# A recommendation tower on one core: copies of 128 rows for the pair products, and squares in quarters of the array

## What is computed

```
conv1 = einsum('bid,bjd,ijk->bkd', e, e, W1)          # 39 x 39 pairs of features -> 128
hidden1, final1 = conv1[:, :64], conv1[:, 64:]
conv2 = einsum('bid,bjd,ijk->bkd', e, hidden1, W2)    # 39 x 64 -> 128
z = concat([final1, conv2], 1).sum(over d)            # 192 numbers a sample
h = relu(concat([z, dense_ctx]) @ W_top1 + b_top1)    # 208 -> 512
h = relu(h @ W_top2 + b_top2)                         # 512 -> 256
y = h @ W_top3
```

## Time and profile before

| | |
|---|---|
| median of three runs | 795.92 us (795.42 to 796.37) |
| span of the profiled execution | 794.7 us |
| busy: PE, DVE, ACT, POOL | 734.3, 700.8, 634.8, 541.0 us |
| TensorE's clock, mean granted | 0.989 |
| moved by DMA | 169 MB, 213 GB/s over the span |

### The profile page before, as it was taken

How to read it: one execution, slowest core, us unless ns; L and a number is a source line. 1 busy time by engine, 2 the same in 40 slices (tenths; PEclk the granted TensorE clock), 3 DMA queues, 4 the chain that set the end, 5 groups by cost and what they waited for, 6 DMA issues and landing times.

```text
span 794.7 us, 18326 instructions
## 1 busy us (share of the span) xinstructions
PE 734.3 (92%) x6944; PEld 419.2 (53%) x6944; DVE 700.8 (88%) x1142; ACT 634.8 (80%) x1573; POOL 541.0 (68%) x542
## 2 busy tenths in 40 slices
PE   1895869899999999999999999999999999999996
PEld 0552123445556464656556566546455645666576
DVE  6984979989999989999999998998989999999862
ACT  1332459788998988888989989897979889898973
POOL 6887777777777777777777777777777777720000
PEclk9998989999999999999999999999999999999999
DMA  6738888788889788888878896878878788878300
GB/s 194 229 85 268 245 203 237 222 222 227 230 232 261 209 228 241 218 237 236 237 217 247 239 273 169 256 198 242 238 214 252 203 234 242 231 205 255 127 2 2
DMA packets 130904, 168.99 MB, mean 213 GB/s; under 512 B 99144, under 2 KB 112182, under 8 KB 114080
## 3 DMA queue, kind: packets, MB, share of 16 engines
q1 hardware_dynamic: 110756, 156.62, 67.1%
q0 software_dynamic: 16896, 8.68, 7.1%
q10 hardware_dynamic: 3164, 2.52, 1.1%
HBM read 156.03 MB, written 16.71 MB: 217 GB/s over the span
## 4 chain that ended last, share of the span: by engine, by line
DMA 26%; PE 25%; DVE 24%; ACT 13%; SPq 7%; issue 4%; POOL 1%; ACTq 0%; DVEq 0%
DVE blocks L827 20%; DMA copies<-xt 16%; PE hidden L455 9%; DMA emb<-in_tbl,ids_tile 8%; ACT arena L670 6%; PE sums L482 4%; PE hidden L569 4%; SPq L361 4%; PE sums L508 3%; ACT xdiag L658 2%; ACT hid_high L639 2%; DVE turned L859 2%; PE sums L526 2%; SPq L332 2%; ACT copies L688 1%
## 5 line engine op out<-in xcount | busy, mean ns | idle before, releaser
L422 POOL DMA_INDIRECT emb<-in_tbl,ids_tile x528 | 537.8, 1019 | 160.9 <-issue 101.8
L827 DVE TENSOR_TENSOR blocks<-copies 117x512 f32<-117x512 f32 x840 | 524.5, 692 | 57.3 <-DMA copies<-xt 24.0
L455 PE MATMUL hidden<-blocks,w_pairs 117*64 117x512 f32 x1792 | 430.8, 605 | 20.2 <-DVE blocks L827 18.4
L670 ACT ACTIVATE arena<-sums 64x480 f32<-64x480 f32 (+2 forms) x936 | 293.0, 313 | 38.8 <-PE sums L482 24.7
L455 PEld LDWEIGHTS hidden<-blocks,w_pairs 117*64 117x64 f32 x1792 | 144.5, 137 | 231.3 <-DVE blocks L827 113.9
L482 PEld LDWEIGHTS sums<-xdiag,turned 64*103 64x103 f32 x2000 | 99.3, 168 | 90.2 <-issue 54.7
L482 PE MATMUL sums<-xdiag,turned 64*103 64x78 f32 x2000 | 112.9, 257 | 13.2 <-ACT arena L670 10.9
L658 ACT ACTIVATE xdiag<-turned 32x468 f32<-32x468 f32 (+1 forms) x256 | 118.9, 464 | 3.1
L688 ACT ACTIVATE copies<-copies 117x2048 f32<-117x2048 f32 x32 | 61.2, 1912 | 54.4 <-DMA copies<-xt 34.9
L508 PE MATMUL sums<-arena,weights 128*64 128x128 f32 x1280 | 76.7, 275 | 1.3 <-DVE weights L920 1.3
L639 ACT ACTIVATE hid_high<-hidden 32x512 f32<-32x512 f32 x126 | 74.1, 588 | 2.2 <-PE hidden L455 0.3
(11 more groups left out here) (53 smaller groups left out, 292.7 us busy)
## 6 DMA issues: line engine op xcount, KB each, us to landing
copies<-xt SPq DMA_DIRECT2D x416, 312.0 KB
emb<-in_tbl,ids_tile POOLq DMA_INDIRECT x528
xt<-xt SPq DMA_DIRECT2D x16, 304.0 KB, 4.9
xt<-emb SPq DMA_DIRECT2D x30, 152.0 KB
xt<-emb SPq DMA_DIRECT2D x34, 104.0 KB
blocks<-hot_t SPq DMA_DIRECT2D x12, 256.0 KB, 5.5
xt<-emb SPq DMA_DIRECT2D x32, 56.0 KB
weights<-in_finals SPq DMA_DIRECT2D x1, 1728.0 KB, 9.7
```

Source lines behind the costliest of these rows:

```text
L422: pool.indirect_dma_start(out=emb[u][:, f * D:(f + 1) * D], out_offset=None, in_=tables[f], in_offset=bass.IndirectOffsetOnAxis(ap=ids_til ...
L455: mm = nc.tensor.matmul(hidden[64 * c:64 * c + 64, k % 2, bank, :], w_pairs[0:ROWS, t, bank * HALF_HID:bank * HALF_HID + HID], blocks[0:RO ...
L670: op = nc.scalar.activation(out[:, :, cols].rearrange("p h (u b) -> p h u b", u=2), g[rows, i], ACT.Copy)
L827: op = nc.vector.tensor_tensor(blocks[0:ROWS, at + c, :], a[:, cols], b[:, cols], ALU.mult)
```

## The change

Copies 0 to 3 get 128 rows: 117 as before with other rotations, and 11 more rows loaded by a fourth DMA of 11 contiguous rows (88 KB). For copies 0 to 2 these are features 2 to 12, 15 to 25 and 28 to 38, so the products of these copies also hold pairs of features 13 apart, for 11 of each 13. Of the two remaining offsets there are six pairs; for them VectorE adds the two features (`sum_pairs`), SP writes the six sums behind the wrapped rows of `xt` (`write_sums`), and copy 3 has them among its last rows. a*b is then taken from (a+b)^2 - a^2 - b^2, through the weights: half of the pair's weight at the sum, minus half at the two squares.

Copy 4 and step (0, 4) go; there are six product steps (12 ring places a chunk) and a seventh step of squares. Rows 64 to 127 of copy 3 hold every feature and the six sums. ScalarE squares them for bank 0 into partitions 0 to 63 of `squares` (64x1024), VectorE for bank 1 into partitions 64 to 127, and TensorE multiplies in quarters: 64 rows by 64 columns, one half of the rows for each bank.

SP's order: the spill's parts are now features 0 to 22, 23 to 31, 32 to 38 (23 rows are wrapped); part 0 ahead of copy 1, part 1 ahead of copy 3, part 2 behind copy 3, and behind it the two writes of the sums. The sums of tile t+1 are added by VectorE at the end of step t = 6 of chunk 2t, which is behind its products of step 2 of chunk 2t+1.

```diff
-PRODUCTS = [(0, 1), (0, 2), (1, 2), (0, 3), (0, 4), (1, 3), (2, 3)]
-STEPS = len(PRODUCTS)
+PRODUCTS = [(0, 1), (0, 2), (1, 2), (0, 3), (1, 3), (2, 3)]
+SQUARES = len(PRODUCTS)
+STEPS = len(PRODUCTS) + 1
...
-PARTS = [slice(0, 19), slice(19, 32), slice(32, F)]
+PARTS = [slice(0, 23), slice(23, 32), slice(32, F)]
...
-ROTATION = [(0, 0, 0), (1, 2, 5), (4, 10, 12), (15, 19, 18)]
+ROTATION = [(17, 11, 0), (18, 21, 15), (23, 23, 19), (9, 0, 22)]
...
+            def write_sums(tile):
+                u = tile % 2
+                sp.wait_ge(sums_ready, tile + 1)
+                for h in range(2):
+                    sp.dma_start(
+                        xt[u, SUMS_AT:XROWS, h, :].rearrange("f (s d) -> s f d", d=D),
+                        sum_x[u][h::2, :].rearrange("s (f d) -> s f d", d=D),
+                    ).then_inc(sums_written[u], 16)
...
+                if len(PARTS) - 1 in some:
+                    write_sums(tile)
                 if tile + 2 < TILES and len(PARTS) - 1 in some:
                     next_ids(p, u)
...
                 for v in LOAD_ORDER:
-                    if v in SPILL_AT and k == 1 and chunk // 2 + 1 < TILES:
-                        spill((chunk // 2 + 1) // 2, 1 - u, [SPILL_AT.index(v)])
+                    if v in SPILL_AT and spills:
+                        spill(after, 1 - u, [SPILL_AT.index(v)])
                     load_copy(p, u, k, v)
+                if spills:
+                    spill(after, 1 - u, [len(PARTS) - 1])
...
-                if v == 4:
-                    sp.wait_ge(squares_set, chunk + 1)
-                elif since(chunk, ahead):
-                    sp.wait_ge(multiplied, pairs_done(chunk - ahead, COPY_USES[v][-1], BANKS - 1))
+                if since(chunk, 2):
+                    sp.wait_ge(multiplied, pairs_done(chunk - 2, COPY_USES[v][-1], BANKS - 1))
...
-                for g in LOADED[v]:
-                    r = ROTATION[v][g]
-                    sp.dma_start(x_copy[v][k % ahead][g::THIRDS, :],
-                                 xt[u, r:r + F, k, :]).then_inc(copied[v][k % ahead], 16)
+                if v == 3:
+                    if since(chunk, 2):
+                        sp.wait_ge(squared_low, chunk - 1)
+                        sp.wait_ge(squared_high, chunk - 1)
+                    if k == 0:
+                        sp.wait_ge(sums_written[u], 32 * (p + 1))
+                for g, r in enumerate(ROTATION[v]):
+                    sp.dma_start(x_copy[v][k][g:ROWS:THIRDS, :], xt[u, r:r + F, k, :]).then_inc(copied[v][k], 16)
+                at = EXTRA_FROM[v]
+                sp.dma_start(x_copy[v][k][ROWS:P, :], xt[u, at:at + EXTRA, k, :]).then_inc(copied[v][k], 16)
...
+                if t == SQUARES:
+                    for bank in range(BANKS):
+                        pe.wait_ge([squared_low, squared_high][bank], chunk + 1)
+                        rows = slice(LOW * bank, LOW * bank + LOW)
+                        for c in range(2):
+                            mm = nc.tensor.matmul(hidden[64 * c:64 * c + 64, k % 2, bank, :],
+                                                  w_pairs[rows, t, bank * HALF_HID:bank * HALF_HID + HID],
+                                                  squares[rows, chunk % 2, c, :], start=False, stop=True)
...
-            def set_squares(k, tile, chunk):
-                act.wait_ge(copied[0][k % 2], loads_done(0, tile, k % 2))
-                if since(chunk, 1):
-                    act.wait_ge(multiplied, pairs_done(chunk - 1, COPY_USES[4][-1], BANKS - 1))
-                nc.scalar.activation(x_copy[4][0], x_copy[0][k % 2], ACT.Copy).then_inc(squares_set, 1)
+            def square_low(k, tile, chunk):
+                act.wait_ge(copied[3][k % 2], loads_done(3, tile, k % 2))
+                if since(chunk, 2):
+                    act.wait_ge(hid_squares, squares_done(chunk - 2, 0))
+                nc.scalar.activation(squares[0:LOW, chunk % 2], two_slices(x_copy[3][k % 2], 0)[LOW:P],
+                                     ACT.Square).then_inc(squared_low, 1)
...
-                        if t == 3 and chunk + 1 < CHUNKS:
-                            set_squares((k + 1) % 4, 2 * p + (k + 1) // 2, chunk + 1)
+                        if t == 3:
+                            square_low(k, tile, chunk)
...
+            def sum_pairs(tile):
...
+                n = TAKEN * D
+                thirds = emb[u][:, :].rearrange("p (a f) -> p a f", a=3)[:, :, 0:n]
+                sums_of = sum_x[u][:, :].rearrange("p (e f) -> p e f", f=n)
+                nc.vector.tensor_tensor(sums_of[:, 0:2], thirds[:, 0:2], thirds[:, 1:3], ALU.add)
+                nc.vector.tensor_tensor(sums_of[:, 2], thirds[:, 0], thirds[:, 2], ALU.add).then_inc(sums_ready, 1)
+
+            def square_high(p, k):
...
+                x = two_slices(x_copy[3][k % 2], 1)[LOW:P]
+                nc.vector.tensor_tensor(squares[LOW:P, chunk % 2], x, x, ALU.mult).then_inc(squared_high, 1)
...
-                            op = nc.vector.tensor_tensor(blocks[0:ROWS, at + c, :], a[:, cols], b[:, cols], ALU.mult)
+                            op = nc.vector.tensor_tensor(blocks[:, at + c, :], a[:, cols], b[:, cols], ALU.mult)
...
+                        if t == LAST and k % 2 == 0 and not (last_pair and k == 2):
+                            sum_pairs(2 * p + k // 2 + 1)
```

More of the change, by code:

```diff
@@ L116, in build @@
         gst = [turned[:, u] for u in range(2)]
-        copies = sb("copies", [P, 2 * COPIES - 1, COLS], F32)
-        x_copy = [[copies[0:ROWS, 4 * s + u if u < 4 else 8, :] for s in range(2 if u < 4 else 1)] for u in range(COPIES)]
+        sum_x = [sb(f"sum_x{u}", [P, SUM_ROWS * D], F32) for u in range(2)]
+        copies = sb("copies", [P, 2 * COPIES, COLS], F32)
+        x_copy = [[copies[:, COPIES * s + u, :] for s in range(2)] for u in range(COPIES)]
+        squares = sb("squares", [P, 2, 2, SLICE], F32)
         blocks = sb("blocks", [P, 2 * RING, SLICE], F32)
@@ L201, in build @@
         spilled = [sem(f"spilled{u}") for u in range(2)]
-        squares_set = sem("squares_set")
+        sums_ready = sem("sums_ready")
+        sums_written = [sem(f"sums_written{u}") for u in range(2)]
+        squared_low = sem("squared_low")
+        squared_high = sem("squared_high")
         copied = [[sem(f"copied{u}_{s}") for s in range(len(x_copy[u]))] for u in range(COPIES)]
@@ L236, in pairs_done, with squares_done @@
             return PAIRS_A_CHUNK * chunk + BANKS * t + bank + 1
+        def squares_done(chunk, bank):
+            return BANKS * chunk + bank + 1
         def strides_of(tile):
             sums, layers = 2 * THIRDS, 2 * 2
-            return PAIRS_A_TILE + N_GROUPS * (1 if tile == 0 else 2) + (sums if tile else 0) + (layers if since(tile, 2) else 0)
+            return 2 * (PAIRS_A_CHUNK + 1) + N_GROUPS * (1 if tile == 0 else 2) + (sums if tile else 0) + (layers if since(tile, 2) else 0)
         def strides_until(tile):
@@ L400, in first_tile @@
                 for v in LOAD_ORDER:
+                    if v == 3:
+                        write_sums(0)
                     load_copy(0, 0, 0, v)
@@ L971, in layouts @@
              for h in range(2) for r in range(2 * GROUPS[j]) for q in range(2)]
-    numbers = np.full((P, 18), -1, "float32")
+    numbers = np.full((P, 19), -1, "float32")
+    numbers[:, 18] = 0
     for at, c in (0, 8), (8, 10):
@@ L979, in layouts @@
     W2 = W2.reshape(F, HID, CONV2)[ORDER].reshape(F * HID, CONV2)
-    pairs = np.zeros((2, ROWS, STEPS, HID + HALF_HID), "float32")
+    both = np.concatenate([w1[:, :, 0:HID], w1[:, :, 0:HALF_HID]], 2)
+    pairs = np.zeros((P, STEPS + SQUARES + HALVES, HID + HALF_HID), "float32")
     for t, (u, v) in enumerate(PRODUCTS):
-        for g in range(min(len(ROTATION[u]), len(ROTATION[v]))):
-            for i in range(F):
-                a, b = (i + ROTATION[u][g]) % F, (i + ROTATION[v][g]) % F
-                for side, row in enumerate([w1[a, b], w1[b, a]][0:1 if a == b else 2]):
-                    pairs[side, THIRDS * i + g, t, 0:HID] = row[0:HID]
-                    pairs[side, THIRDS * i + g, t, HID:] = row[0:HALF_HID]
+        feature = [[(i + r) % F for i in range(F) for r in ROTATION[w]] + list(range(EXTRA_FROM[w], EXTRA_FROM[w] + EXTRA)) for w in (u, v)]
+        for row, (a, b) in enumerate(zip(*feature)):
+            if row < ROWS or v < 3:
+                pairs[row, t], pairs[row, STEPS + t] = both[a, b], both[b, a]
+    rows_of = {}
+    for row in range(LOW, ROWS):
+        rows_of.setdefault((row // THIRDS + ROTATION[3][row % THIRDS]) % F, row)
+    for half in (0, LOW):
+        for a, row in rows_of.items():
+            at = row - LOW + half
+            pairs[at, SQUARES] = both[a, a]
+            near = [e[0] if e[1] == a else e[1] for e in SUMMED if a in e]
+            for n, b in enumerate(near):
+                pairs[at, STEPS + SQUARES + 2 * n], pairs[at, STEPS + SQUARES + 2 * n + 1] = both[a, b], both[b, a]
```

(5 more changed lines are left out.)

104 lines of the change are left out of this document (69 added, 35 removed).

## The result

The changed kernel is **slower**: 850.95 us median (847.24 to 855.02) against 796.14 us of the kernel before beside it, ratio 1.068 [1.064, 1.072]. The forecast was 793.3 us, with 804 as its upper end; both are missed, and it went as the rival *DMA falls behind* said, at more than four times the price of its example (55 us; "1 us over is 13 us at the end"). A run's time lies 1.8 us above its own span (847.24 and 845.4 in the profiled one), and not 1.2 as read from the kernel before.

The account below looks back on a forecast made before the run. POOL's unbroken gathers until 702.2 us were taken as the bound, 92.5 us following. There +1.2 - 0.5 - 1.8 - 1.5 = -2.6 us gave a 792.1 span, plus 1.2: 793.3 us; range 784 to 804, the forecast's own 790 to 794.3.

Parts of the forecast that it names:

- DMA falls behind: Rival, thirteen tiles between 140 and 700 us: added transfers and SP's later order exceed the room left; slower, chance 0.28.
- 1 us over is 13 us at the end: The DMA rival's example: excess per tile over POOL's 43.3 us adds up, giving 806 us.
- who paced the kernel before: POOL's gathers run without a pause until 702.16 us, 43.3 us a tile; PE's 98% is only nearly as long.
- the engines' durations: Per chunk: VectorE's square 1.2 us, ScalarE's 1.0, TensorE's squares step 0.90, or 1.80 if quarters run one after another.
- no second function table: ScalarE: if Square needed another table than Copy, two loads of 1.28 us a chunk would be added; trace didn't tell.
- I take 1.2: DMA term: added transfer time per tile, 1.1 us by bytes at least, 8 at most; 1.2 us taken.
- 2.2 us of a tile are left: DMA room per tile: share 0.83 against 0.88 while loads are queued, 43.3 x 0.05 = 2.2 us.
- upper bound of 8 us: DMA cost per tile at most, if each of six further loads costs as much as a large one, 1.2 us.
- the sums' wait: SP's queue waits for VectorE's step 2 of the odd chunk: at most 0.9 us late, taken as 0.
- I take 0, with ends -6 and +4: POOL's gathers: fewer multiplies might save 6 us in all, the longer square add 10 against that; net 0 taken.
- the last 92.5 us: Stretch after POOL's last gather: later loads, PE free earlier, shorter squares steps and no gram-copy waits sum to -2.6 us.
- Slower had 0.28: Chance given to a result slower by over 0.2%, all from DMA falling behind, half of it up to 804 us.

Follow-up runs that it names:

- b2: The kernel before with 32 gathers instead of 33 in each tile from the third on: 785.05 us beside 798.02, ratio 0.986.
- b6: The kernel before with eight more eleven-row loads a tile into partitions 117 to 127, from the third tile on: 847.26 us, ratio 1.060.
- b3: The kernel before with the change's eight eleven-row loads a tile added, into rows 117 to 127 that nothing reads: 857.23 us, ratio 1.077.
- b4: The kernel before with eight more eleven-row loads a tile from the third on, rows 12 partitions apart in a scratch: 829.12 us, ratio 1.036.
- b8: The kernel before with eight more spread eleven-row loads a tile from the third on, rows of 4 KB, half the length: 803.82 us, ratio 1.008.
- a1: The changed kernel with VectorE's additions for the sums moved in front of step 0 of the odd chunk: 839.77 us, ratio 1.057.
- c2: The changed kernel with eleven-row loads spread 12 partitions apart from the third tile on and sums added at step 3, not 6: 813.94 us, ratio 1.022.
- a6: The changed kernel with sums added in front of the odd chunk and no eleven-row loads from the third chunk on: 805.78 us, ratio 1.011.
- a8: The changed kernel without eleven-row loads from the third chunk on, VectorE's 64x1024 square cut into two of 64x512: 801.58 us, ratio 1.005.
- a9: The changed kernel without eleven-row loads from the third chunk on, VectorE's square in two and sums added at step 3: 800.04 us, ratio 1.004.
- a4: The changed kernel without the eleven-row loads from the third chunk on, their pairs and sums left out: 804.13 us, ratio 1.008.
- c1: The changed kernel with its eleven-row loads going to partitions 12 apart in a scratch from the third tile on: 827.65 us, ratio 1.041.
- b7: The kernel before with eight more loads a tile from the third on, eleven neighbouring partitions each, eight different groups: 866.85 us, ratio 1.089.
- b5: The kernel before with eight more loads a tile from the third on, sixteen rows of 5632 bytes, 8 partitions apart: 829.79 us, ratio 1.041.

## Why the prediction was wrong

**Right: who paced the kernel before.** POOL without a pause, PE's 98% no bound. One gather less a tile made it 13 us faster; but 0.9 us a tile further the engines behind POOL were the bound (b2), which the prediction did not see.

**Right: the engines' durations,** with a squares step at 1.10 us in place of 0.90, and no second function table. Since none of it lay on the path, their exactness was worth nothing.

**Wrong, and the step that failed: DMA.** "I take 1.2, nearer to the bytes, because an 88 KB load moves 88 KB", held against "2.2 us of a tile are left". The price was too low, and the room was never shown.
- The price. It nets 80 KB: 26 large loads less 24, against eight small ones. The eight measured 0.56 us each where their rows are neighbours (b6), 4.5 us a tile; the two large ones that go give back 2 x 1.2 = 2.4; the wrapped rows and sums, 64 and 96 KB, stay at the 0.25 and 0.5 us that bytes give (not measured alone). Together some 2.8 us, not 1.2 (at a room of 0.9 us; 3.2 at 1.3). The text's own upper bound of 8 us held; the value was taken from the wrong end.
- The room. 0.88 was the share in a stretch of queued loads, and a mean share is no measure of room: 0.85 stands in a kernel whose chain holds the loads (b3) and in one whose chain holds none (b2). The room was at least 0.9 us (b2), by estimate 1.3 (b4, b8); whether 2.2 was wrong stays open.
- So about 1.9 us a tile were over, 26 us in 14 tiles, by DMA alone; this difference is the same for either room. The steps below give 23 + 10 us.

**Wrong: the sums' wait, "at most 0.9 us late, less with a faster VectorE" and "taken as 0".** It was 5.2 us. The time of VectorE's step 2 was read from a trace in which the copies were not late; once they are, VectorE is late, the sums stand behind its products, and all loads of the next tile stand behind the sums: lateness is fed back. It cost 11 us alone (a1) and 14 us with spread rows (c2), and nothing where transfers aren't late (a6).

**Wrong: gathers, "I take 0, with ends -6 and +4".** Without the loads they cost 1036 ns in place of 1019, 528 x 0.017 = 9 us, beyond the bad end. The long square named there as a risk is the cause in a8, and about half of it with the sums early (a9). The Trainium skill's rule (SBUF — State Buffer, Who interferes with whom), by which this term is exactly 0, is spoken against a second time: one VectorE instruction cut in two gave 18 ns a gather back in a8 and 7 in a9.

**Not settled: the last 92.5 us, "-2.6".** In the four versions without the loads (a4, a6, a8, a9), which POOL paces, 91.6, 91.0, 96.9 and 89.9 us follow the last gather, one profile each; they differ by more than the term.

**The steps in one row,** each as its time above the kernel before beside it: the change 54.8 us, rows spread 31.7 (c1), sums earlier 18.0 (c2), no eleven-row loads 7.8 (a6), square in two 3.3 (a9). So neighbouring partitions 23 us, the sums 14, the loads' bytes 10, the long square 4, open 3; the last two are near what these medians can tell. The order matters: sums first are worth 11.

**The chances.** Slower had 0.28, and the range ended at 804 on the strength of "1 us over is 13 us". The multiplication was right; 1 us was a guess inside a bound of 8 us less 2.2.

## What to carry to other kernels

Where two paces lie within a few per cent, measure the room of the second (one unit of work less for the first) before adding to it, and read in the chain of waits whose room it was; a mean share of the queues isn't room. Cost a small load by the partitions it lands in as well as by its bytes, and spread its rows. A wait in an in-order load queue for the engine that those loads feed turns any lateness into more: put its producer several steps earlier than the trace of before asks for.

## What was not expected of the hardware

Eleven rows of 8 KB into neighbouring partitions took 0.56 to 0.74 us of the transfers' time, spread ones 0.39 (with a room of 0.9 us), and eleven rows or sixteen made no difference. SP issued a load of eleven neighbouring rows in 0.52 us (b6, b7), one of eleven rows 12 partitions apart in 0.73 (b4), so the dearer load is the one that is issued faster; sixteen rows 8 apart took 0.53 (b5). And one VectorE instruction of 64x1024 in place of two of 64x512, a chunk, made the mean gather 18 ns longer (1018 to 1036 ns, a8 and a4), and 7 ns with the sums early (a9 and a6).
